# Weighing all fourteen slots on VectorE, and the nodes' old and own parts with them, in a two-layer graph attention kernel

## The reference

```python
h = (h_in @ W).reshape(n, Hh, Cc)
alpha_s = jnp.sum(h * a_s, axis=-1)
alpha_d = jnp.sum(h * a_d, axis=-1)
e = jax.nn.leaky_relu(alpha_s[src] + alpha_d[dst], 0.2)
m = jax.lax.stop_gradient(jax.ops.segment_max(e, dst, num_segments=n))
ex = jnp.exp(e - m[dst])
alpha = ex / jax.ops.segment_sum(ex, dst, num_segments=n)[dst]
out = jax.ops.segment_sum(h[src] * alpha[:, :, None], dst, num_segments=n)
return out.reshape(n, Hh * Cc) + b
```

## Time and profile before

| | |
|---|---|
| median of 3 runs | 4242.11 us (4241.45 to 4245.93) |
| the profiled execution | 4241.65 us |
| its span, first to last instruction | 4239.8 us |
| busy: VectorE / GpSimd / TensorE / ScalarE | 84% / 72% / 65% / 53% |
| gathers, whole execution | 3136 = 2 layers x 112 steps x 14 |

### The profile page before, as it was taken

How to read it: one execution, slowest core, us unless ns; L and a number is a source line. 1 busy time by engine, 2 the same in 40 slices (tenths; PEclk the granted TensorE clock), 3 DMA queues, 4 the chain that set the end, 5 groups by cost and what they waited for, 6 DMA issues and landing times.

```text
span 4239.8 us, 55419 instructions
## 1 busy us (share of the span) xinstructions
PE 2746.8 (65%) x9786; PEld 1883.8 (44%) x9786; DVE 3551.8 (84%) x12391; ACT 2259.7 (53%) x7167; POOL 3063.3 (72%) x3188
## 2 busy tenths in 40 slices
PE   6666666666666666666665666666666666666666
PEld 4444444444444444444443444444444444444444
DVE  5678888888888888888867888888888888888888
ACT  4445555555555555555553555555555555555555
POOL 3277777777777777777747777777777777777774
PEclk9877777777777777777776777777777777777777
DMA  7455555555555555555535555555555555555553
GB/s 215 154 143 151 150 150 151 150 150 150 150 151 150 151 150 150 150 148 149 148 106 145 158 158 158 157 158 158 158 158 157 158 157 155 157 159 157 157 157 102
DMA packets 325448, 645.46 MB, mean 152 GB/s; under 512 B 97250, under 2 KB 194954, under 8 KB 325306
## 3 DMA queue, kind: packets, MB, share of 16 engines
q0 software_dynamic: 151008, 429.04, 37.6%
q1 hardware_dynamic: 128520, 171.76, 13.6%
q10 hardware_dynamic: 45890, 44.36, 3.0%
HBM read 597.18 MB, written 47.71 MB: 152 GB/s over the span
## 4 chain that ended last, share of the span: by engine, by line
POOL 55%; issue 22%; PE 13%; DMA 5%; DVE 3%; ACT 0%; POOLq 0%; DVEq 0%; SPq 0%; ACTq 0%
POOL rows_all L490 55%; PE bank L1086 10%; DMA rows_all<-table,edge 4%; PE bank L1036 1%; PE bank L1094 1%; PE bank L1108 1%; DMA table<-row 1%; DVE stats L738 1%; DVE rows_all L847 0%; DVE ahead L858 0%; PE bank L1073 0%; DMA xg<-in_x_dram 0%; DVE value L852 0%; DVE hnT L760 0%; PE bank L1024 0%
## 5 line engine op out<-in xcount | busy, mean ns | idle before, releaser
L490 POOL DMA_INDIRECT rows_all<-table,edge x3136 | 3023.4, 964 | 1125.0 <-issue 1104.6
L1086 PE MATMUL bank<-rows_all,onehot 128*128 128x264 f32 x6272 | 1872.7, 457 | 19.7 <-DVE rows_all L847 9.9
L1086 PEld LDWEIGHTS bank<-rows_all,onehot 128*128 128x128 f32 x6272 | 1384.1, 228 | 459.5 <-DVE rows_all L847 186.1
L561 ACT ACTIVATE rows_all<-rows_all 128x64 f32<-128x64 f32 x3584 | 878.3, 337 | 3.7
L1068 PE MATMUL bank<-onehotT,logit_p 128*128 128x448 bf16 x896 | 260.5, 423 | 679.0 <-DVE logit_p L838 679.0
L847 DVE TENSOR_TENSOR rows_all<-rows_all,bank 128x768 f32<-128x768 f32 (+1 forms) x672 | 658.8, 1037 | 0.0
L1073 PE MATMUL bank<-ident,ahead 128*4 128x128 f32 x224 | 83.9, 374 | 725.2 <-DVE behind L860 725.2
L573 ACT ACTIVATE share<-node_d 128x8 f32<-128x8 f32 x224 | 46.7, 209 | 872.5 <-DVE node_d L916 872.5
L867 DVE TENSOR_TENSOR onehot<-bank,dloc 128x1792 f32<-128x1792 f32 x224 | 453.5, 2024 | 7.7
L1068 PEld LDWEIGHTS bank<-onehotT,logit_p 128*128 128x128 bf16 x896 | 76.9, 106 | 826.9 <-DVE logit_p L838 770.7
L852 DVE COPY value<-rows_all 128x56 f32<-128x56 f32 x224 | 58.4, 261 | 438.4 <-DMA rows_all<-table,edge 438.4
(11 more groups left out here) (170 smaller groups left out, 3634.8 us busy)
## 6 DMA issues: line engine op xcount, KB each, us to landing
dst_b<-dst_row SPq DMA_DIRECT2D x224, 448.0 KB, 3.9
rows_all<-table,edge POOLq DMA_INDIRECT x3136
self_row<-table SPq DMA_DIRECT2D x224, 132.0 KB
table<-row ACTq DMA_DIRECT2D x113, 132.0 KB
x_row<-in_x_dram SPq DMA_DIRECT2D x112, 128.0 KB, 2.2
out_dram<-y_out ACTq DMA_DIRECT2D x112, 128.0 KB
table<-row ACTq DMA_DIRECT2D x24, 528.0 KB, 3.8
xg<-in_x_dram SPq DMA_DIRECT2D x24, 512.0 KB, 3.6
```

The source lines that it names most:

```text
L490: nc.gpsimd.indirect_dma_start(out=G[u][:, j, :], out_offset=None, in_=table[L][0:N, :], in_offset=bass.IndirectOffsetOnAxis(ap=index[:, j ...
L561: last = nc.scalar.activation(G4[t.u][:, j, h, 0:C], G4[t.u][:, j, h, 0:C], ACT.Copy, scale=G4[t.u][:, j, h, C:C + 1])
L1086: last = nc.tensor.matmul(bank[3 + t.half][:, 0:ROW], onehot[t.half][:, j, :], G[t.u][:, j, :], start=(j == 0), stop=(j == SLOTS - 1))
```

## The change

VectorE now weighs all 14 slots, in three parts of 5, 5 and 4 slots where it weighed 10 in parts of 4, 3 and 3; `weigh_last` and its semaphore are gone. `old_part` and `own_part` are made by one VectorE instruction each where ScalarE used four each. ScalarE keeps `share`, the exponentials, moves, stores and GELU. TensorE sums in three parts.

```diff
-    PARTS = [(0, 4), (4, 7), (7, 10), (10, SLOTS)]
-    DVE_PARTS = 3
+    PARTS = [(0, 5), (5, 10), (10, SLOTS)]
...
-            def weigh_last(t):
-                t0, t1 = PARTS[DVE_PARTS]
-                act.wait_ge(s["wcol_ready"], t.done(0))
-                for j in range(t0, t1):
-                    for h in range(H):
-                        last = nc.scalar.activation(G4[t.u][:, j, h, 0:C], G4[t.u][:, j, h, 0:C], ACT.Copy,
-                                                    scale=G4[t.u][:, j, h, C:C + 1])
-                last.then_inc(s["act_weighted"], 1)
...
                 nc.scalar.activation(share[:], node_d[:], ACT.Exp).then_inc(s["share_ready"], 1)
-                act.wait_ge(s["share_ready"], t.done(0))
-                for h in range(H):
-                    last = nc.scalar.activation(old_part[:, h, :], bank[5][:, h * HW:h * HW + C + 1], ACT.Copy, scale=share[:, 1, h:h + 1])
-                last.then_inc(s["old_part_ready"], 1)
-                for h in range(H):
-                    last = nc.scalar.activation(own_part[:, h, :], self_row[t.u][:, h * HW:h * HW + C], ACT.Copy, scale=share[:, 0, h:h + 1])
-                last.then_inc(s["own_part_ready"], 1)
...
             def node_totals(t):
                 S = bank[3 + t.half][:, 0:ROW].rearrange("p (h c) -> p h c", h=H)
+                old = bank[5][:, 0:ROW].rearrange("p (h c) -> p h c", h=H)
+                dve.wait_ge(s["share_ready"], t.done(0))
+                nc.vector.tensor_tensor(old_part[:], old[:, :, 0:C + 1], wide(share[:, 1], 2, C + 1), ALU.mult).then_inc(s["old_part_ready"], 1)
                 dve.wait_ge(s["old_part_ready"], t.done(0))
...
                 nc.vector.tensor_tensor(weight[:], total[:, :, C], share[:, 0], ALU.add).then_inc(s["weight_ready"], 1)
+                nc.vector.tensor_tensor(own_part[:], self_row[t.u][:].rearrange("p (h c) -> p h c", h=H)[:, :, 0:C], wide(share[:, 0], 2, C), ALU.mult
+                                        ).then_inc(s["own_part_ready"], 1)
                 dve.wait_ge(s["own_part_ready"], t.done(0))
...
-                    for nth in range(DVE_PARTS):
+                    for nth in range(len(PARTS)):
                         weigh(weighed, nth)
...
-                pe.wait_ge(s["act_weighted"] if part == DVE_PARTS else s["weighted"][part], t.done(0))
+                pe.wait_ge(s["weighted"][part], t.done(0))
...
                     sum_up(weighed, 2)
-                    sum_up(weighed, 3)
```

More of the change, by code:

```diff
@@ L233, in two_layer_graph_attention @@
                      "carryT_done of_node_ready known_ready reach_ready reached_ready max_ready pre_ready logit_ready fall_ready "
-                     "w_ready wcol_ready wmax_ready act_weighted sum_done weight1_ready weightr_ready mmax_ready absent_ready emax_ready total_max_ready "
+                     "w_ready wcol_ready wmax_ready sum_done weight1_ready weightr_ready mmax_ready absent_ready emax_ready total_max_ready "
                      "self_z_ready old_z_ready max_z_ready node_l_ready node_d_ready no_old_ready old_max_ready least_max_ready share_ready old_part_ready own_part_ready "
@@ L238, in two_layer_graph_attention @@
         s = {n: sem(n) for n in step_sems}
-        s["weighted"] = [sem(f"weighted{k}") for k in range(DVE_PARTS)]
+        s["weighted"] = [sem(f"weighted{k}") for k in range(len(PARTS))]
         for n in "edge_landed mark_landed self_landed x2_landed landed".split():
@@ L613, in act_body @@
                     move_actT(stored_)
-                if weighed:
-                    weigh_last(weighed)
                 if finished:
@@ L1087, in sum_up @@
                                             start=(j == 0), stop=(j == SLOTS - 1))
-                if part == DVE_PARTS:
+                if part == len(PARTS) - 1:
                     last.then_inc(s["sum_done"], 1)
```

## The result

The changed kernel takes 4284.28 us (median of 4 runs, 4283.08 to 4287.0) against 4242.17 us before (4 runs, 4241.45 to 4245.93). The ratio is 1.0099, with a 95% interval from 1.0084 to 1.0113: slower by 42 us, 1%. 4290 was forecast, with 4265 to 4325 as its range.

What follows compares the result with a forecast made beforehand. The prediction took GpSimd, issuing gathers back to back, to bound the kernel in both layers. The profiled 4241.65 us plus 45 for layer 2 and 3 for layer 1 gave 4290 us, range 4265 to 4325.

Steps and rivals of the forecast that it cites:

- The weighing, +1.06: VectorE's three weighing instructions handle 3584 elements in a partition where they handled 2560: 1.06 us a step more.
- The parts, +0.45 each: On VectorE, one multiply each for `old_part` and `own_part`, with a dependence behind it: 0.45 us a step each.
- Layer 2, VectorE 0.41 us over the room, +45: VectorE's added 1.96 us exceeds its room of 1.55 us by 0.41 us in each of 111 steps: +45 us.
- Layer 1, GpSimd stays the bound, +3: VectorE's added 1.96 us stays under its room of 2.07 us; GpSimd sets the step, 0.03 us more each: +3 us.
- GpSimd gets slack and waits for TensorE in each step of layer 2: GpSimd runs ahead, uses up its slack after some 14 steps, then waits for TensorE's sums each step; adds nothing.
- ScalarE, TensorE, SyncE at nothing: ScalarE's removed rows, TensorE's sums ending 0.3 us later and SyncE's wait some 4 us later in the body cost nothing.
- The drains, zero within 1 us: Two stretches of last steps without gathers: 0.26 us more at the sums, some 1 us less between `share` and `summed`.
- C: Rival: the added work fits VectorE's room, its sum under 1.55 us a step; no change, 4242 us; chance 0.08.
- B: Rival: VectorE bounds both layers, small multiplies costing 0.6 us each, sum 2.3 us a step; 4350 us; chance 0.09.
- R: Rival: `own_part` holds a gather in every step, 0.42 us each, 47 us in layer 1; 4334 us; chance 0.08.
- D: Rival: without ScalarE's removed rows VectorE's rows shorten, gathers go undelayed at 17.50 us a step; 58 us less, 4184; chance 0.04.

Runs made afterwards that it cites:

- the last experiment: The kernel before with `old_part` and `own_part` on VectorE and the one-hot of the nodes (`onehotT`) on ScalarE: 4216.53 us.
- experiment 59: Not a run's number: 59 counts gathers in the kernel of the last experiment, which took 4216.53 us.

## Why the prediction was right, and where it was not

**The weighing, +1.06.** The weighing alone moved took 1.99 - 0.92 = 1.07 us of the idle a step in layer 1. Right.

**The parts, +0.45 each.** 0.42 us a row and 0.034 us of dependence behind it. The sum is 1.99 us with 0.01 more in each of the two dependent rows (425 ns, where 419 and 418 were expected), against 1.96.

**Layer 2, VectorE 0.41 us over the room, +45.** The mechanism was right and the size a little high. The step rose from 17.74 to 18.07 us, 0.33, and 0.33 x 111 is 37 us, of which 31.9 stand between the gathers and 5.2 behind the last one. The term that was off is the body of before: `value` took 299 ns there while it waited for gathers and takes 202 ns now, so 0.10 us of what was counted as VectorE's own work went with the wait.

**Layer 1, GpSimd stays the bound, +3.** This step failed, though its number (+3.8) came out. VectorE bounds layer 1 too: no idle before `value`, VectorE's step is 17.83 us where its own rows should have needed 17.67, and a row more makes it longer. `onehotT` grew by 65 ns and `value` by 40, as more of them start where GpSimd holds them, and the sum was 0.03 us larger: 17.67 + 0.03 + 0.07 + 0.04 = 17.81. What the forecast treated as a fixed body is stretched by the gathers. GpSimd, which was to stay the bound at 17.78, could by its own gathers have gone at 17.75. That the two errors, a wrong bound and a body too short, gave +3.8 beside +3 is luck. So the total, 4284 against 4290, is right by its main term, layer 2's, and not by this one.

**GpSimd gets slack and waits for TensorE in each step of layer 2.** Half right. Its waits between 2330 and 4150 us, after:

```profile
POOL rows_all L489 <- issue: 436.2, 1380, 1.6
POOL rows_all L489 <- PE bank L1072: 18.0, 33, 1.3
```

Before, no wait for TensorE there was over 0.3 us. Now 33 add up to 18.0 us, the longest 1.3, and some of its "issue" gaps reach 1.6 us as well. With 32 gaps over 0.4 us in some 100 steps, GpSimd is held in every third step or so, not in each.

**ScalarE, TensorE, SyncE at nothing.** Right: VectorE's idle for the exponential is 1.4 us and for `share` 1.1 us in the whole execution. No wait of SyncE shows on the chain.

**The drains, zero within 1 us.** Mis-sized. The drain between the layers is 2.7 us longer and the end behind the last gather 5.2 us, since VectorE, now the bound, is further behind the gathers when these end: the last `value` of layer 1 starts 3.4 us after its last gather's end where it was 1.9, and that of layer 2 6.0 us where it was 2.0. That is 1.5 and 4.0 us of the two; the rest isn't traced.

**The rivals.** C (it fits) is what happens to each half alone; B (both layers VectorE) is right in its bound and wrong in its price, since its dear small multiplies aren't there. R named contention, which is real with 0.03 to 0.16 us a step; `own_part` does hold gathers, but has the smaller part in it. D was right that gathers without holds give 17.5 us a step and wrong that this change brings them.

The Trainium skill ("SBUF — State Buffer", "Who interferes with whom") says that a VectorE instruction with two SBUF inputs contends with a GpSimd instruction that reads SBUF. The traces agree: it is what happens to the 58 gathers beside `summed` in the kernel before, and in the kernel of the last experiment 59 gathers that start beside `own_part` end 0.81 to 0.82 us after its end. They also show more than that sentence names: `onehotT` and `value`, each with a single tensor in SBUF as input, hold gathers or are held by them. The Trainium skill ("SBUF — State Buffer", "Summary: rules for kernel authors") says that the second one to issue fully blocks until the first finishes. The traces agree on that for gathers that start beside `summed`. A hold costs little all the same, since most of the row is over when the gather comes to need SBUF: 0.06 to 0.16 us there, and at most 0.48 us (1.43 against 0.946 us) in the kernels before and after. So the prediction's price for R, a hold of the row's whole 0.42 us in each step, was too high twice: a hold is shorter, and 59 gathers in 224 steps are not one in each.

## What to carry to other kernels

Work out an engine's room where it waits for the pacemaker (the engine that sets the step), in each stage apart, and compare the whole added work with it: two edits that are each free can cost 42 us together. Work belongs on the engine with real room, here ScalarE, and what to take away from VectorE first is the rows that collide with the pacemaker, not the cheapest ones to move. When the forecast leaves a margin of a tenth of a us, treat the stage as bound by both engines and expect each to stretch the other.

## What the runs showed of the hardware

- VectorE rows and gathers hold each other: `onehotT` takes 0.66 us or up to 0.89 us, a gather 0.945 us or up to 1.43 us, by the moment at which they meet. A gather that starts beside `summed` or `own_part` (two inputs in SBUF each) ends 0.81 to 0.82 us after that row does. Started 0.3 to 0.5 us into a gather, `onehotT` stretched it to 1.23 us on average; started 0.5 to 0.8 us into it, `onehotT` itself took 0.86 us. Moving that one row off VectorE brought 46 us.
- An indirect gather of 128 rows of 264 fp32 values costs GpSimd 0.945 us and 0.305 us behind it: 17.50 us for 14, and 17.52 was the shortest step measured.
- ScalarE makes 1792 columns in 1.78 us (int16 to bf16) and 1.70 us (bf16 to bf16), some 1.0 ns a column, where VectorE's `is_equal` makes them in 0.66 us undisturbed.
